# Attention and the seam to the last MLP: GpSimd's query-weight subtraction waits for the rotation, and another order of steps on all engines

## The reference, cut to what matters

```python
# attention: 32 query heads, 8 key/value heads of 128; 4 query heads share one key head
q = (hidden_states @ Wq.T)...;  q = q * cos + _rotate_half(q) * sin
scores = einsum(q, k) * scale;  attn = softmax(where(causal, scores, -1e9))
return (attn @ v) @ Wo.T
# MLP: each weight is base + mean(|w - base|) * sign(w - base)
h = silu(x @ W1.T) * (x @ W3.T);  return h @ W2.T
```

## Time and profile before

| | before |
|---|---|
| median of 3 runs (lowest, highest) | 1866.13 us (1865.6, 1867.11) |
| the profiled execution: its own time | 1867.5 us |
| its span, first to last instruction | 1865.7 us |
| busy share of PE, DVE, ACT, POOL | 90, 60, 47, 44% |
| mean granted clock of PE | 0.968 of full |
| attention groups | about 985 to 1592 us |
| seam to the last MLP | about 1560 to 1646 us |

### The profile page before, as it was taken

The page is one execution under the profiler, slowest core; times in us unless marked ns, Lnnn a source line. Parts: engine busy times, 40 slices in busy tenths (PEclk is TensorE's granted clock), DMA queues, the critical chain, the costliest instruction groups (busy, mean ns, idle before and its releaser), DMA issues. The chain is left out here.

```text
span 1865.7 us, 24304 instructions
## 1 busy us (share of the span) xinstructions
PE 1676.6 (90%) x8214; PEld 1377.9 (74%) x8214; DVE 1114.2 (60%) x1592; ACT 872.7 (47%) x1761; POOL 818.6 (44%) x416
## 2 busy tenths in 40 slices
PE   5994899999997799897998999999999998799988
PEld 4851787777876688676877787788787877678867
DVE  4326999999997522343725666666666667632232
ACT  2336767676764444232623454444444545433231
POOL 2201888888885464142612222222322224355353
PEclk9997999999999999898998999999999999999989
DMA  3102001010100097001201000100100010134100
GB/s 111 63 1 76 41 21 47 12 56 0 68 0 24 1 364 277 18 1 34 63 25 44 23 23 23 45 22 22 45 22 22 22 57 35 69 135 145 59 18 28
DMA packets 25188, 100.84 MB, mean 54 GB/s; under 512 B 3104, under 2 KB 3360, under 8 KB 22560
## 3 DMA queue, kind: packets, MB, share of 16 engines
q1 hardware_dynamic: 24976, 99.89, 14.9%
q10 hardware_dynamic: 144, 0.07, 0.0%
HBM read 97.72 MB, written 2.23 MB: 54 GB/s over the span
## 5 line engine op out<-in xcount | busy, mean ns | idle before, releaser
L985 PE MATMUL psum<-scratch_s,res_const 128*128 128x256 f32 x1024 | 247.5, 380 | 3.8 <-DVE scratch_s L957 3.8
L1615 POOL TENSOR_TENSOR stretch_turned<-stretch_turned,res_const 128x1024 f32<-128x1024 f32 x32 | 80.3, 2509 | 386.8 <-ACT stretch_turned L1476 386.8
L985 PEld LDWEIGHTS psum<-scratch_s,res_const 128*128 128x128 f32 x1024 | 194.1, 190 | 32.0 <-DVE scratch_s L957 5.8
L858 POOL TENSOR_TENSOR scratch_s<-scratch_s,scan_cm 128x1024 f32<-128x1024 f32 x64 | 150.9, 2358 | 54.2 <-DVE scratch_s L947 54.2
L947 DVE TENSOR_TENSOR_SCAN scratch_s<-psum,scratch_s 128x512 f32<-128x512 f32 x128 | 155.5, 1214 | 4.4 <-ACT psum L899 4.2
L1339 PE MATMUL psum<-opnd_xh,query_wqh 128*128 128x256 f32 x512 | 151.3, 296 | 1.9 <-PEq L94 1.9
L846 POOL TENSOR_TENSOR scratch_s<-scan_bm,scratch_s 128x1024 f32<-128x1024 f32 x64 | 151.0, 2360 | 0.1
L899 ACT ACTIVATE psum<-ssm_dt,ssm_vec 128x255 f32 (+1 forms) x256 | 111.2, 466 | 80.4 <-DVE scratch_s L947 79.9
L1339 PE MATMUL psum<-opnd_xh,query_wql 128*128 128x256 f32 x512 | 145.7, 284 | 0.0
L1339 PE MATMUL psum<-opnd_xl,query_wqh 128*128 128x256 f32 x512 | 145.5, 284 | 0.0
L1484 ACT ACTIVATE stretch_pa<-psum,stretch_nm 128x128 f32<-128x128 f32 x128 | 45.3, 366 | 196.7 <-DVE stretch_nm L1706 196.7
(11 more groups left out here) (269 smaller groups left out, 4322.3 us busy)
## 6 DMA issues: line engine op xcount, KB each, us to landing
mi_dw<-in_dw SPq DMA_DIRECT2D x24, 448.0 KB, 5.5
mi_dm<-in_dm SPq DMA_DIRECT2D x24, 448.0 KB, 6.2
query_raw<-in_w_q SPq DMA_DIRECT2D x8, 1024.0 KB, 4.7
query_raw<-in_w_o SPq DMA_DIRECT2D x8, 1024.0 KB, 4.7
scan_cm<-bc_rows SPq DMA_DIRECT2D x12, 512.0 KB, 4.0
gu_raw<-in_w_gu SPq DMA_DIRECT2D x11, 512.0 KB, 7.3
mlpa_raw<-in_w_mlp SPq DMA_DIRECT2D x7, 768.0 KB, 4.2
mlpa_base<-in_b_mlp SPq DMA_DIRECT2D x7, 768.0 KB, 5.7
```

Source lines behind the costliest of these rows:

```text
L858: nc.gpsimd.tensor_tensor(shared[r][h], shared[r][h], weights(4 * h, 4), ALU.mult).then_inc(weighted_pool, 1)
L985: mm = nc.tensor.matmul(ps_y[r], ident, part[:, n * SEQ:(n + 1) * SEQ], start=False, stop=stop and (n + 1) * SEQ == part.shape[1])
L1615: nc.gpsimd.tensor_tensor(heads(turned[:, :]), heads(turned[:, :]), over_heads(C_SIN, SEQ), ALU.mult).then_inc(q_sine, 1)
```

## The change

GpSimd gets a wait before the subtraction of the query weights (L1619): until the rotation of the next unit's queries is done. In the last group (b = 2) it gets a wait for the last rotation as well, and difference(1) moves from before the two residuals to behind mlp_low(0). At the seam the order of the steps changes on PE, ACT, POOL and DVE. Apart from the two waits no step is added and none is taken out; whole_down(0) and (1) move to earlier places.

```diff
--- before.py
+++ after.py
@@ -1441,20 +1441,20 @@
             weights_split(0)
             pe.wait_ge(exped, U)
             widen_batch(0, 0)
+            token_transposes(2)
+            token_transposes(3)
             weights_split(1)
             widen_batch(1, 0)
-            token_transposes(2)
-            token_transposes(3)
-            widen_batch(0, 1)
             token_transposes(4)
             token_transposes(5)
+            widen_batch(0, 1)
             widen_batch(1, 1)
             pe.wait_ge(added, 2 * U)
             widen_batch(2, 2)
             token_transposes(6)
+            token_transposes(7)
             pe.wait_ge(half_kept, 1)
             widen_batch(3, 2)
-            token_transposes(7)
             widen_batch(2, 3)
             widen_batch(3, 3)
             for f in range(2, F1):
@@ -1562,6 +1562,8 @@
                 for t, x in ((0, X[2]), (1, X[0])):
                     act.wait_ge(summed, v * 2 + t + 1)
                     nc.scalar.activation(oh[:, t, :], x, ACT.Copy).then_inc(o_hi, 1)
+                    if ending(g, b, BATCH - 1) and t == 0:
+                        y_norm(2)
                 if b == 0:
                     output_weights(g)
                 if more(g, b):
@@ -1574,7 +1576,6 @@
             groups(act, body)
             token_high(0)
             token_high(1)
-            y_norm(2)
             y_norm(3)
             mlp_high(1)
             y_norm(4)
@@ -1583,21 +1584,21 @@
             x_norm(3)
             token_high(2)
             token_high(3)
+            x_norm(4)
+            x_norm(5)
             y_norm(6)
             y_norm(7)
-            x_norm(4)
-            x_norm(5)
             token_high(4)
             token_high(5)
             gate_half(0)
             x_norm(6)
             x_norm(7)
+            gate_half(1)
             token_high(6)
-            gate_half(1)
             token_high(7)
             difference_sign(2)
+            mlp_high(2)
             gate_half(2)
-            mlp_high(2)
             gate_half(3)
             difference_sign(3)
             mlp_high(3)
@@ -1648,30 +1649,32 @@
                 if more(g, b):
                     sine(*after(g, b))
                 if b == 2 and not (isinstance(g, int) and g == GROUPS - 1):
+                    pool.wait_ge(q_done, g * BATCH + b + 2)
                     query_weights(g + 1)
                 if b == 0:
                     output_weights(g)
                 if ending(g, b, 0):
                     difference(0)
                 if ending(g, b, 2):
-                    difference(1)
+                    pool.wait_ge(q_done, U)
                     residual(0)
                     residual(1)
                     mlp_low(0)
+                    difference(1)
 
             sine(0, 0)
             groups(pool, body)
             x_scale(0)
             y_scale(1)
-            y_scale(2)
             residual(2)
             residual(3)
+            y_scale(2)
+            mlp_low(1)
             x_scale(1)
             residual(4)
             residual(5)
-            mlp_low(1)
+            y_scale(3)
             x_scale(2)
-            y_scale(3)
             residual(6)
             residual(7)
             x_scale(3)
@@ -1799,7 +1802,10 @@
                 dve.wait_ge(flipped, v * 3 + 2)
                 nc.vector.tensor_copy(pt[:, 1, :], X[0]).then_inc(p_kept_dve, 1)
                 if last:
+                    x_shift(0)
                     y_moments_of(1)
+                    whole(1)
+                    y_shift(1)
                 if more(g, b):
                     rotate(*after(g, b))
                 for t, x in ((0, X[2]), (1, X[0])):
@@ -1813,12 +1819,12 @@
                     y_shift(0)
                 if ending(g, b, 2):
                     values(g, b + 1, v + 1)
+                    whole_down(0)
                     accumulate(v, b)
-                    x_moments_of(0)
                 if more(g, b):
                     probabilities(*after(g, b))
                 if ending(g, b, 2):
-                    x_shift(0)
+                    x_moments_of(0)
 
             nc.vector.memset(flat(acc), 0.0).then_inc(zeroed, 1)
             dve.wait_ge(zeroed, 1)
@@ -1827,37 +1833,34 @@
             maxima(0, 0)
             probabilities(0, 0)
             groups(dve, body)
-            y_shift(1)
             y_moments_of(2)
             token_low(0)
             token_low(1)
-            whole(1)
             y_shift(2)
             x_moments_of(1)
+            whole_down(1)
+            x_shift(1)
             accumulate(U - 1, BATCH - 1)
             y_moments_of(3)
-            x_shift(1)
             x_moments_of(2)
+            y_shift(3)
+            x_shift(2)
             token_low(2)
             token_low(3)
-            y_shift(3)
-            x_shift(2)
-            whole_down(0)
-            whole_down(1)
-            x_moments_of(3)
             token_low(4)
             token_low(5)
+            x_moments_of(3)
+            x_shift(3)
             keep_half(0)
-            x_shift(3)
+            keep_half(1)
             token_low(6)
-            keep_half(1)
             token_low(7)
             whole(2)
             whole_down(2)
             keep_half(2)
+            keep_half(3)
             whole(3)
             whole_down(3)
-            keep_half(3)
             for f in range(2, F1):
                 if f >= 3 and f + 1 < F1:
                     whole(f + 1)
```

## The result

| | before | after |
|---|---|---|
| median (lowest to highest), us | 1866.62 (1865.6 to 1867.84) | 1846.55 (1845.7 to 1847.19) |
| ratio of the medians, 95% interval | | 0.9892 (0.9877 to 0.9908) |
| the profiled execution: time, span | 1867.5, 1865.7 | 1847.19, 1845.4 |
| mean granted clock of PE | 0.968 | 0.969 |

A forecast was written before the change was run, and what follows sets the result against it. PE is busy for 90% of the span, so time is won only where it idles or runs at half clock. 8.0 + 1.7 + 0.0 (parts 2 and 3) + 8.1 - 0.6 = 17.2 us off 1866.13: 1849 us, range 1843 to 1857.

The forecast's parts named there:

- part 1: Attention loop, seven units: rotation freed from GpSimd's subtraction, half returning as a wait for low weights; 8.0 us plus 1.7 clock.
- part 2: GpSimd's order in the last group: rotation no longer held, transposes at about 1585.0 instead of 1586.46; 1.4 us gained.
- part 3: DVE and ACT steps moved ahead of the last output product: it starts at about 1594.1, losing the 1.4 us.
- part 4: New order behind the last output product: 14.1 us of waits and clock fall to 6; 8.1 us, less 0.6.
- half clock in group 5: PE at 0.83 of its clock after the loop wait; taken as gone for 1.7 us, between 0 and 1.7.
- The forecast's wait of 1.2 us: Loop: PE would wait seven times about 1.2 us for the low query weights from GpSimd's L1619.
- Rival C: Loop: PE's wait for low weights outgrows the one removed, +14 us in seven units; 1872 us, chance 0.04.
- rival D: Loop subtraction of some 6.5 us, only the half clock won at the seam: no change, 1866 us; chance 0.03.
- Rival B: Low weights don't hold PE back, or the seam closes better: part 1 up to 16.2, 1841 to 1843; chance 0.06.
- of 1.85 us 0.5 to 0.8 are left: Last group: the earlier scores' gain shrinks because the small L1706 is held behind difference(1) until 1579.1 to 1579.4.
- My own list of new waits: Behind the last output product: 2.8 for token_transposes(2), 1.5 and 1.1 for x_norm, 1.0 for mlp_low(2), short ones; 6 us.
- the walk: New order behind the last output product stepped through with the rows' durations: x_norm(2) ends at 1605.1, PE through at 1602.4.

The follow-up runs named there:

- e1: The kernel before with only GpSimd's loop wait ahead of the query weights' subtraction added: 1855.73 us, ratio 0.9948.
- e9: The kernel before with only GpSimd's order of the last unit as in after (wait for the rotation, difference(1) behind mlp_low(0)): 1862.31 us, ratio 0.9984.
- e3: The kernel before, no new wait, with the query weights' subtraction (L1619) as two instructions of 1024 columns: 1850.42 us, ratio 0.9912.
- e2: The kernel after without the loop wait, so only the last group and the seam are new: 1854.41 us, ratio 0.9942.
- e8: The kernel before with only POOL's new seam order (mlp_low(1) and the scales as in after): 1863.2 us, ratio 0.9983.
- e6: The kernel after with PE's seam order put back as in before: 1852.64 us, ratio 0.9932.
- e11: The kernel after with y_shift(1) and whole(1) on DVE back behind the groups and y_norm(2) on ACT back: 1848.57 us, ratio 0.9903.
- e4: The kernel after with the query weights' subtraction in two halves in place of the loop wait: 1838.55 us, ratio 0.9851.

## Why the prediction was right, and where it was off

| | predicted | measured (profiled executions) |
|---|---|---|
| part 1, loop | 8.0 + 1.7 | 8.98 (e1): 7.3 + 1.7 |
| part 2, up to the last transposes | 1.4 | 1.8 in after, 2.0 in e9 |
| part 3, up to the last output product | -1.4 | -0.3 |
| part 4, behind it | 8.1 - 0.6 | 9.2 |
| sum | 17.2 | 19.7, and 0.5 ahead of the attention |

**Part 1: right, in mechanism and size.** The rotation is at 1.22 us everywhere (1225 ns at most), PE waits for the low weights instead, and half clock in group 5 is gone. That it went for its full 1.7, out of a stated 0 to 1.7, was a choice that came true, not something derived. The gain per unit is 1.04 instead of 1.14. Two small terms work against it: the subtraction takes 4.52 us, and from its end to PE it is 0.36 us in the six loop groups, where I had put 0.13 from a signal of VectorE, 0.25 together. From L1386 to the first query matmul a unit is 0.92 us shorter (5.61 before, 4.69 after). The rest is won right behind: the second query matmul follows the first after 0.19 us instead of 0.31, and counted to it the unit is 1.04 us shorter. The forecast's wait of 1.2 us was measured as 1.05. Rival C needed weights later than 1351.0 in the earlier trace rows's unit, that is a subtraction over 5.6 us long, and rival D one of some 6.5; it took 4.52. Rival B had the low weights in time; e3 reached that by other means, and got 16.6 us from the first scores to the last, the 1.7 of the clock included.

**Part 2: the hold was right, the balance wrong.** L1709 was held for 1.20 us behind difference(1), as forecast. The step that failed is "of 1.85 us 0.5 to 0.8 are left" with only a bit added for x_moments_of(0). I had the hold eat into the gain. But in before the reciprocals waited for x_moments_of(0) and not for the exponentials, so the hold only took up time that was already lost (10.61 against 10.62 us from scores to reciprocals, and 10.60 in e9). The whole shift of the scores came through, 1.8 to 2.0.

**Part 3: the loss was over-estimated, and the clock hid part of it.** PE's last output product starts 1583.05 - 1575.14 = 7.91 us after the transposes; I had 9.1, and before has 7.62. The timeline of DVE in after:

```profile
1577.76 0.15 DVE L1754 SCALAR_TENSOR_TENSOR stretch_ln<-stretch_ln 128x2 f32<-128x2 f32 x1
1577.83 1.28 DVE L1731 BATCH_NORM_STATS2 stretch_ln<-acc_acc 128x6 f32<-128x512 f32 x2
...
1579.44 1.41 DVE L1765 SCALAR_TENSOR_TENSOR mlpb_raw<-mlpb_raw,res_coeff,mlpb_base 128x512 f32<-128x512 f32 x2
1580.77 0.16 DVE L1740 SCALAR_TENSOR_TENSOR stretch_ln<-stretch_ln 128x2 f32<-128x2 f32 x1
1580.85 0.68 DVE L1813 TENSOR_TENSOR stretch_ol<-psum,stretch_oh 128x512 fp32r<-128x512 f32 x1
```

x_shift(0) starts 2.6 us after the transposes, as I had it. The term that was mis-sized is whole(1): I added 0.7 us to its 1.41 for POOL's y_scale(1) between its halves, and DVE lost nothing there; POOL did the waiting:

```profile
1579.61 1.13 POOL L1628 TENSOR_TENSOR stretch_ln<-stretch_ln,res_half 128x2 f32<-128x2 f32 x1 [2.12 <-DVE stretch_ln L1736]
```

The rest, 0.5 us, is in small instructions that follow each other more closely than the sum of their durations. PE's wait before the product stayed at 0.5 us, where I had 1 to 3. In e2, with less time at the lower clock level, the same order made PE wait 1.56 us, and the product came 1.0 us later behind the transposes than with the order of before (7.89 against 6.89 and 6.94). So the small loss of 0.3 is in part the luck of a stretch that was slow for PE anyway.

**Part 4: right in kind, 1.7 too low.** I took 14.1 us as what could be won, 12.4 of waits and 1.7 of clock. My own list of new waits, 2.8 + 1.5 + 1.1 + 1.0 and some short ones, comes to 6.4 and more, and I wrote 6; the term should have been 7.7 at most. Of the waits 3.4 are left, not 6: no short gaps between paired transposes, and 2.5 instead of 5.4 us for x_norm, in two waits of 1.83 and 0.66. The first of them in PE's timeline of after:

```profile
1593.49 1.82 PE L1396 MATMUL psum<-res_const,norm_xn 128*128 128x128 f32 x8 [1.83 <-ACT norm_xn L1509]
```

That is 10.4 us after the last output product, where the walk had 11.0, and PE arrived 8.6 us after it, where the walk had 8.3: together 0.9 us less of waiting. Half clock struck once more, as I had allowed for with 0.6; the windows of after:

```profile
1590.00:1600.00 10.00, 8.12 (x54) 7.47 (x54) 7.78 (x19) 4.76 (x8) 5.00 (x5) 0.83 0.43 159
1605.00:1615.00 10.00, 9.29 (x77) 8.85 (x76) 7.88 (x8) 4.35 (x6) 3.61 (x2) 1.00 0.01 2
```

Before had its 0.83 at 1605 to 1615, behind the wait of 4.6 us; now it is behind the wait of 1.83, for as long. So the clock gave nothing here, and the part's 9.2 us is 12.4 - 3.4 = 9.0 of waits. The detailed holds of the walk were right: y_shift(2) stood 2.04 us behind mlp_low(1), x_shift(1) 1.21 behind residual(4). One that I had not walked, x_shift(3) behind difference(2), was 3.45 us and led to no wait of PE over 0.7.

Which of the engines' new orders earns part 4 was not in the prediction. By e8, e6 and e11: POOL's order alone 3.2; in the whole, PE's order 6.1; whole(1) and y_norm(2) together 2.0 by the medians and 1.25 by the traces, within the noise. That they do not simply add up is to be expected, since PE's early transposes should only pay if x_norm is early, which needs DVE's and POOL's order; PE's order without the others was not run.

The four parts erred by 0.4 to 1.7 us each, and the sum came out 2.5 us too low in the traces and 2.9 in the medians. Part 1 was 0.7 too high and the other three together 3.2 too low, so a little of the agreement is cancellation.

## What to carry to other kernels

GpSimd's subtractions of 2.4 to 4.6 us held certain VectorE instructions to their end, even one on two columns (3.45 us behind difference(2)). Before giving GpSimd a wait, try cutting its instruction: here two halves were worth 8.0 us more than the wait (e4 against after), since VectorE gets in between them and PE has to wait for neither. And in a stretch where four engines wait for each other in turn, move the consumer's order together with the producer's: POOL's order alone was worth 3.2 us, all engines' together 9.2.

## What the runs showed of the hardware that I had not expected

- Not all of VectorE's SBUF work was held. Held beside GpSimd's subtractions were TENSOR_TENSOR and SCALAR_TENSOR_TENSOR with all operands in SBUF, and TENSOR_SCALAR on 2 and 8 columns. Operations with an operand in PSUM kept their 0.69 us, and so did the layernorm's statistics, which read the tokens from SBUF; this one of before runs beside mlp_low(1), two instructions in 1.27 us:

```profile
1604.91 1.27 DVE L1742 BATCH_NORM_STATS2 stretch_ln<-tok_x 128x6 f32<-128x512 f32 x2
```

- Two GpSimd instructions back to back let a waiting VectorE instruction in between them: the pair took 5.66 us instead of 4.50, the rotation 2.25 instead of 4.41 (e3). In the other direction it was a stand-off without cost for VectorE: whole(1)'s two instructions stayed at 1.41 us while GpSimd's two-column instruction took 1.13 instead of 0.70. Whether that one ran between the halves or beside the second is open.
- From the end of GpSimd's subtraction to PE's next matmul it was 0.36 us in the loop (1124.50 to 1124.86), where from VectorE's rotation to PE it was 0.14. It is not GpSimd that is slow to tell: the same subtraction in group 0, outside the loop, was followed after 0.10 us, and mlp_low(2) at widen(2, 0) after 0.14 (1620.26 to 1620.40). PE has several waits ahead of the queries, and in the loop their counts depend on the group; that they make the difference is likely, but no run tests it.
- Of the seven units in which PE stood idle for 1.75 or 2.05 us the granted clock fell in one, in group 5, and in the same one in every kernel that has these waits (before, e2, e8, e9); after the idle times of 1.05 us in e1 and after it did not. At the seam it fell behind a wait of 1.83 (after), and behind one of 1.88 in e8 but not behind the same one of 1.91 in before and 1.88 in e1. So a wait taken away can bring up to 1.7 us more than its length, and these runs do not show how to tell beforehand when it does.
- Around the same wait of some 4.5 us at the last transposes PE was at the lower level for 3.4 us in four executions (e1, e2, e3, e9) and for 6.8 in the others, which moved the last output product by some 0.7 us (6.9 us behind the transposes in e1 and e9, 7.6 in before, with the same code there).
